# First FFN weight block of an attention and quantized-FFN kernel: four tiles converted in place and turned by transposing transfers during the last two batches

## The reference

```python
def _L0_xattn_ref(query, key):
    a = jnp.einsum('bqd,bkd->bqk', query, key)
    e = jax.nn.softmax(a, axis=-1)
    return jnp.einsum('bqk,bkd->bqd', e, key)
...
    w = _dequantize(qweight, weight_scale, weight_zero_point)   # (v - zero_point) * scale
    return jnp.einsum('bsk,nk->bsn', x, w) + bias
...
    x = x + jnp.tanh(g_xattn[0]) * _L0_xattn_ref(_layernorm(x, axis=-1), ctx_4096)
    x = x + jnp.tanh(g_ffn[0]) * _L0_ffn_ref(_layernorm(x, axis=-1), ...)
    return x
```

## Time and profile before

| | us |
|---|---|
| median of three runs | 578.82 |
| lowest, highest | 577.61, 582.05 |
| the profiled execution | 578.77 |
| its span, first to last instruction | 577.0 |
| PE busy | 565.8 (98%) |
| DVE busy | 358.7 (62%) |
| ACT busy | 287.5 (50%) |
| POOL busy | 214.7 (37%) |
| SP's queue, share of 16 DMA engines | 66.3% |

### The profile page before, as it was taken

The page is one execution under the profiler, slowest core; times in us unless marked ns, Lnnn a source line. Parts: engine busy times, 40 slices in busy tenths (PEclk is TensorE's granted clock), DMA queues, the critical chain, the costliest instruction groups (busy, mean ns, idle before and its releaser), DMA issues.

```text
span 577.0 us, 8618 instructions
## 1 busy us (share of the span) xinstructions
PE 565.8 (98%) x3390; PEld 407.1 (71%) x3390; DVE 358.7 (62%) x684; ACT 287.5 (50%) x447; POOL 214.7 (37%) x187
## 2 busy tenths in 40 slices
PE   7989999999999999999999999999999999999997
PEld 7879969968968977987986996665554444444445
DVE  5577717826836745755673782966949665655443
ACT  3667567568666676765765757545431220210000
POOL 3046178169249339429619709912000000000000
PEclk9999999999999999999999999999999999999999
DMA  7999749327828727747755675788996994962311
GB/s 237 277 321 240 215 149 305 98 81 239 255 86 274 262 84 265 257 119 220 247 173 177 246 236 229 252 304 279 243 233 208 211 260 134 196 161 71 86 55 42
DMA packets 49203, 115.79 MB, mean 201 GB/s; under 512 B 27960, under 2 KB 28216, under 8 KB 40546
## 3 DMA queue, kind: packets, MB, share of 16 engines
q1 hardware_dynamic: 49052, 114.41, 66.3%
q10 hardware_dynamic: 110, 0.82, 0.5%
HBM read 89.26 MB, written 19.66 MB: 189 GB/s over the span
## 4 chain that ended last, share of the span: by engine, by line
PE 85%; DMA 8%; DVE 5%; issue 1%; ACT 1%; SPq 0%
PE S L1161 19%; PE S L1051 13%; PE T L1005 10%; PE pv L1089 8%; PE S L1089 8%; PE S L1053 7%; PE pv L1161 7%; PE pv L1005 6%; DMA raw<-in_ctx 3%; DMA raw<-late 3%; PE pv L1102 3%; PE S L1102 3%; DVE xres L779 3%; DMA xa<-in_x 1%; DVE qT L897 1%
## 5 line engine op out<-in xcount | busy, mean ns | idle before, releaser
L505 POOL TENSOR_TENSOR vlo<-raw,vhi 128x2048 fp32r<-128x2048 f32 (+1 forms) x38 | 174.3, 4614 | 54.9 <-ACT vhi L571 54.9
L1051 PE MATMUL S<-khi,qT 128*100 128x362 f32 x512 | 141.4, 357 | 0.0
L1053 PE MATMUL S<-klo,qT 128*100 128x362 f32 x256 | 85.1, 332 | 0.3
L907 DVE TENSOR_TENSOR klo<-T,khi 128x361 fp32r<-128x361 f32 x128 | 65.9, 529 | 25.1 <-ACT khi L560 24.4
L907 DVE TENSOR_TENSOR klo<-pv,khi 128x361 fp32r<-128x361 f32 x128 | 65.2, 527 | 22.5 <-ACT khi L560 22.0
L560 ACT ACTIVATE khi<-T 128x361 fp32r<-128x361 f32 x128 | 58.6, 475 | 34.8 <-PE T L1005 34.5
L571 ACT ACTIVATE vhi<-raw 128x2048 fp32r<-128x2048 f32 (+1 forms) x38 | 71.9, 1908 | 6.9 <-PE S L1089 6.9
L560 ACT ACTIVATE khi<-pv 128x361 fp32r<-128x361 f32 x128 | 58.5, 476 | 28.3 <-PE pv L1005 28.3
L1161 PE MATMUL S<-raw 128*128 128x512 f16 x320 | 71.6, 379 | 0.0
L1005 PE MATMUL T<-ident,raw 128*128 128x128 f32 (+1 forms) x416 | 64.2, 268 | 3.8 <-DMA raw<-in_ctx 2.5
L1051 PEld LDWEIGHTS S<-khi,qT 128*100 128x100 f32 x512 | 67.7, 167 | 0.0
(11 more groups left out here) (130 smaller groups left out, 740.5 us busy)
## 6 DMA issues: line engine op xcount, KB each, us to landing
raw<-in_ctx SPq DMA_DIRECT2D x24, 1024.0 KB, 10.3
raw<-in_L_ffn_qweight SPq DMA_DIRECT2D x16, 768.0 KB, 8.2
raw<-in_ctx SPq DMA_DIRECT2D x12, 840.0 KB, 10.6
rows_scratch<-xres SPq DMA_DIRECT2D x8, 800.4 KB
xres<-in_x SPq DMA_DIRECT2D x8, 800.0 KB
x_scratch<-xres SPq DMA_DIRECT2D x8, 800.0 KB
raw<-in_ctx SPq DMA_DIRECT2D x12, 512.0 KB, 12.6
late<-x_scratch SPq DMA_DIRECT2D x24, 256.0 KB, 4.3
```

The source lines that it names most:

```text
L505: pool.tensor_tensor(vlo[0:r, k, :], raw[0:r, b % 2, t, 0:D], vhi[0:r, k, :].bitcast(F32), ALU.subtract).then_inc(s_vlo, 1)
L907: dve.tensor_tensor(klo[:, slot, 0:GW], T[k][:, 0:GW], khi[:, slot, 0:GW].bitcast(F32), ALU.subtract).then_inc(s_free[k], 1)
L1051: pe.matmul(into[0:R, g, 0:MW], qT[:, h, c, :], khi[:, slot, :], start=(c == 0 and h == 0), stop=False)
L1053: last = pe.matmul(into[0:R, g, 0:MW], qT[:, 0, c, :], klo[:, slot, :], start=False, stop=(c == CH - 1))
```

## The change

Block 0 now goes the way of the other blocks. ACT converts each of its four tiles in place, where DVE unpacked it, and SP turns it into `WT[0]` by a transposing transfer. PE's 64 transposes, their identity matrix in half precision and ACT's eight copies are gone. Tiles 2 and 3 are unpacked into the third part of `consts`, so the zero points, which belong there, are loaded only when those two tiles are turned, and DVE unpacks tile 2 ahead of the lower half of row tile 0 and tile 3 ahead of that of row tile 1. ACT converts tile 0 behind the last batch's exponentials, tile 1 behind its turned probabilities, tiles 2 and 3 on either side of the first upper half of row tile 1.

```diff
+        def unp_at(n):
+            if n in (2, 3):
+                return consts[:, 2, (n - 2) * 1024:(n - 1) * 1024].bitcast(U16).rearrange("p (j g) -> p j g", j=4)
+            return unp[n % 2]
...
         def wn_at(n):
             k = n % 2
+            if n < RT:
+                return unp_at(n).rearrange("p j g -> p (j g)").bitcast(F16)
...
+        def converted(n):
+            return n + 1
+        def turned_at(n):
+            return 16 * (n // RT + 1)
...
             def weights_turned(n):
                 nb, rt = divmod(n, RT)
-                if nb >= 2:
+                if nb == 0:
+                    used(LAST - 1, 4)
+                    used(LAST - 1, 5)
+                elif nb >= 2:
                     sp.wait_ge(s_y, (nb - 1) * MT)
-                sp.wait_ge(s_wn, n - RT + 1)
+                sp.wait_ge(s_wn, converted(n))
                 sp.dma_start_transpose(WT[nb % 2][:, :, rt * P:(rt + 1) * P], wn_at(n)).then_inc(s_wt[rt], 16)
...
-            sp.dma_start(cB, wzero.rearrange("n o -> (n o)").partition_broadcast(P)).then_inc(s_cB, 16)
             load_rows(1)
             rows_out(LAST - 2)
+            for n in range(3):
+                weights_turned(n)
             x1_out(LAST - 1)
             next_xres(LAST)
             used(LAST, 2)
             load_rows(2)
             load_w(RT)
+            weights_turned(3)
             load_rows(3)
             load_w(RT + 1)
             rows_out(LAST - 1)
+            for n in (2, 3):
+                sp.wait_ge(s_wt[n], turned_at(n))
+            sp.dma_start(cB, wzero.rearrange("n o -> (n o)").partition_broadcast(P)).then_inc(s_cB, 16)
             load_rows(4)
...
                 exps(i + 1)
+                if i + 1 == LAST:
+                    weights_exact(0)
...
                     probs(LAST)
+                    weights_exact(1)
                     ln2_norm(i - 1)
                     rows_hi(0, 1)
                 context_hi(i + 1, 1)
             context_hi(LAST, 2)
-            weights(0)
-            weights(1)
+            weights_exact(2)
             rows_hi(1, 0)
+            weights_exact(3)
             rows_hi(1, 1)
-            weights(2)
             ln2_norm(LAST - 1)
-            weights(3)
...
+                    if n in (2, 3):
+                        dve.wait_ge(s_scores, B)
+                    elif n in (RT, RT + 1):
+                        dve.wait_ge(s_wt[n - RT], turned_at(n - RT))
...
+            unpack(2)
             rows_lo(0, 0)
             probs_lo(LAST)
             rows_lo(0, 1)
             residual(LAST - 1)
             ln2_stats(LAST - 1)
-            unpack(2)
+            unpack(3)
             rows_lo(1, 0)
-            unpack(3)
             rows_lo(1, 1)
...
                 if m == 0:
-                    for f in range(2):
-                        if nb == 0:
-                            written("W", nb * RT + RT - 1, f)
-                    if nb >= 1:
-                        for k in range(RT):
-                            pe.wait_ge(s_wt[k], 16 * nb)
+                    for k in range(RT):
+                        pe.wait_ge(s_wt[k], turned_at(nb * RT + k))
...
-            attend(LAST, {0: lambda: weights(0), 1: lambda: weights(1), 2: lambda: normed(1, (0, 1)),
-                          3: lambda: normed(1, (2, 3)), 4: lambda: weights(2), 5: lambda: weights(3)})
+            attend(LAST, {2: lambda: normed(1, (0, 1)), 3: lambda: normed(1, (2, 3))})
```

More of the change, by code:

```diff
@@ L92, in flamingo_block @@
         ident = sb("ident", [P, P])
-        ident16 = sb("ident16", [P, P], F16)
         fold = sb("fold", [P, 32])
@@ L238, in flamingo_block @@
                 fill("x", 0, 2, 2)
-        for n in range(2):
-            fill("W", n, 2)
         fill("x", 1, 4)
-        for n in range(2, RT):
-            fill("W", n, 2)
         fill("x", 2, 4)
@@ L461, in _ @@
             pool.memset(ident[:, :], 0.0).then_inc(s_id0, 1)
-            pool.memset(ident16[:, :], 0.0).then_inc(s_id0, 1)
             pool.memset(half[:, :], -0.5).then_inc(s_half, 1)
[L464 to L467, removed]
+            pool.wait_ge(s_id0, 1)
+            pool.affine_select(out=ident[:, :], in_=ident[:, :], compare_op=ALU.not_equal, fill=1.0,
+                               base=0, pattern=[[-1, P]], channel_multiplier=1).then_inc(s_id, 1)
             pool.memset(fold[:, :], 0.0).then_inc(s_fold, 1)
@@ L638, in weights_exact @@
                     act.wait_ge(s_pv, B * NCH)
-                elif n not in (2 * RT, 2 * RT + 1):
-                    act.wait_ge(s_wt[(n - 2) % RT], 16 * ((n - 2) // RT))
+                elif n >= RT and n not in (2 * RT, 2 * RT + 1):
+                    act.wait_ge(s_wt[(n - 2) % RT], turned_at(n - 2))
                 act.wait_ge(s_u, n + 1)
-                act.activation(wn_at(n), unp[n % 2].rearrange("p j g -> p (j g)").bitcast(F16), ACT.Copy,
+                act.activation(wn_at(n), unp_at(n).rearrange("p j g -> p (j g)").bitcast(F16), ACT.Copy,
                                bias=-float(BIAS16)).then_inc(s_wn, 1)
@@ L826, in unpack_piece @@
                         lo_made(dve, LAST - 1, 1)
-                    if 2 <= n < RT + 2:
-                        bk, u = bank("W", n - 2, 1)
-                        dve.wait_ge(s_turned[bk], u + 1)
+                    if n in (2, 3):
+                        dve.wait_ge(s_scores, B)
+                    elif n in (RT, RT + 1):
+                        dve.wait_ge(s_wt[n - RT], turned_at(n - RT))
                     elif n >= RT + 2:
-                        dve.wait_ge(s_wn, n - 2 - RT + 1)
-                    dve.tensor_scalar(unp[n % 2][:, 1, :], p[:, :, 0, 0], 6, 63, ALU.logical_shift_right,
+                        dve.wait_ge(s_wn, converted(n - 2))
+                    dve.tensor_scalar(unp_at(n)[:, 1, :], p[:, :, 0, 0], 6, 63, ALU.logical_shift_right,
                                       ALU.bitwise_and).then_inc(s_u1, 1)
@@ L835, in unpack_piece @@
                     j, w = ((0, 0), (2, 1), (3, 2))[k - 1]
-                    dve.tensor_scalar(unp[n % 2][:, j, :], p[:, :, w, 0], 63, 0x6400, ALU.bitwise_and, ALU.bitwise_or)
+                    dve.tensor_scalar(unp_at(n)[:, j, :], p[:, :, w, 0], 63, 0x6400, ALU.bitwise_and, ALU.bitwise_or)
                 else:
                     dve.wait_ge(s_u1, n + 1)
-                    dve.tensor_scalar(unp[n % 2][:, 1, :], unp[n % 2][:, 1, :], 0x6400, None,
+                    dve.tensor_scalar(unp_at(n)[:, 1, :], unp_at(n)[:, 1, :], 0x6400, None,
                                       ALU.bitwise_or).then_inc(s_u, 1)
@@ L1117, in normed @@
                                      for j in range(n) for q, gb in [divmod(n * f + j, G4 // P)]])
-            def weights(n):
-                if n == 0:
-                    pe.wait_ge(s_id, 2)
-                pe.wait_ge(s_u, n + 1)
-                for f in range(2):
-                    k, u = bank("W", n, f)
-                    pe.wait_ge(s_free[k], u)
-                    for c in range(8 * f, 8 * f + 8):
-                        q, gb = divmod(c, G4 // P)
-                        last = pe.transpose(T[k][:, :].bitcast(F16)[:, (c % 8) * P:(c % 8 + 1) * P],
-                                            unp[n % 2][:, q, gb * P:(gb + 1) * P].bitcast(F16), ident16[:, :])
-                    last.then_inc(s_turned[k], 1)
             def multiply(nb, m, between={}):
```

4 lines of the change are left out of this document (removed).

## The result

The kernel after takes 594.32 us (median of 6 runs, 592.04 to 596.74) against 581.48 us for the kernel before beside it (577.61 to 583.13): a ratio of 1.0245, 95% interval 1.021 to 1.028, so 2.5% slower. The forecast was 592.0 us, in a range of 578 to 602: 13.3 us added to 578.8, where 12.8 were measured over 581.48. The profiled execution of after took 592.98 us with a span of 591.2.

The account below looks back on a forecast made before the run. PE and SP's DMA queue were taken as bounds. Four transfers at 3.6 us (14.4) plus 3.0 for cB less 5.1 of filled gaps gave 12.3; with 1.0 start shift, 578.8 + 13.3 = 592 us, range 578 to 602.

Parts of the forecast that it names:

- two limits: PE, busy 98% of the span, and SP's one DMA queue, side by side in the kernel before.
- Gate A: Ahead of the first FFN matmul, PE waits 7 to 11 us for all four transposing transfers of block 0.
- the walk: SP's queue followed in issue order with a price per transfer, from the load of rows 1 issued at 359.71 us.
- start shift: At the queue's start, DVE's unpacking of tile 2 and POOL's steps hold each other up: 0 to 3 us, 1.0 taken.
- Gate B: At row tile 5, ACT's conversion of tile 7 waits for its late transposing transfer; PE stands about 5 us more.
- The price of a transposing transfer: Service in SP's queue for each 512 KB transposing transfer: 3.6 us, range 2.4 to 4.0.
- cB at 3.0 us: Late 1 MB load of the zero points in SP's queue, counted as 3.0 us of added delay.
- rival 4: PE's clock falls in the new gaps, adding 2 to 5 us behind Gate B: 594 to 597 us; chance 0.13.
- The 3.5 us that PE saves: PE drops four batches of 16 transposes before the first FFN matmul, 3.5 us in all, possibly eaten by small delays.
- Hidden: SP's queue takes block 0's transfers in its free engines, so not slower: 575.3 to 574.1 us; chance 0.12.
- No dearer than plain bytes: Each transposing transfer in SP's queue costs 1.5 us, as plain bytes do: 583.7 us; chance 0.13.
- Only gate A: The queue catches up before row tile 5, so only the first FFN matmul's wait counts: 586 us; chance 0.12.

Follow-up runs that it names:

- experiment 3: Kernel after, but weight tiles 2 and 3 of block 0 turned by PE and copied by ACT again: 590.07 us, 1.0186 to before.
- experiment 8: Kernel after with the zero points loaded into 16 of 128 partitions, 128 KB instead of 1 MB: 596.69 us, 1.032 to before.
- experiment 5: Kernel after with block 0's four transposing transfers replaced by plain copies: 590.51 us with 4 KB runs, 595.15 us with 256-byte runs.
- experiments 1 and 2: Kernel after, first with ACT making row tile 5's upper halves before converting weight tile 7, 589.64 us; then with block 0's fourth transposing transfer issued earlier, 592.79 us.
- experiment 6: Kernel after with useless matmuls, 36 before block 0 and 17 at row tile 5: 595.01 us; second run, the 17 moved to where PE stands: 595.83 us.

## Why the prediction held, step by step

- **The two limits and the two gates**: right. Gate A, forecast at 7 to 11 us, is 8.45, and opens at 394.39 - 0.48 = 393.9 on before's clock, the time the walk gave for T3 (394.9 with the start shift). Gate B, forecast at some 5 us, is 4.03; T5 was to land at 434.6 + 1.0 and did at 434.8. On T5's landing and so the end the sum said 13.3; measured are 12.4 behind the mark on the landing and 1.3 for the clock.
- **The price of a transposing transfer**, 3.6 us each in a range of 2.4 to 4.0: right for the queue as a whole up to T4, but not where the walk put it. T4 lands 14.1 us later behind the mark than in before (413.17 and 427.74, less the marks), just the 13.1 of the walk and the 1.0 of the start. But T2 was issued at 371.96 and landed 4.2 us later (the shortest landing of all), so by the prices of the walk it was served until 374.3 and the queue was free of rows 1 and rows out 5 at 367.2, which leaves 7.1 us for three, 2.4 each, the lower bound. And input 7, by the same prices due at 382.4, came at 388.2, in DVE's timeline:

```profile
388.20 1.41 DVE L792 SCALAR_TENSOR_TENSOR xres<-pv,soft,xres 100x512 f32<-100x512 f32 x2 [7.13 <-DMA xres<-in_x]
```

  The delay is in the plain transfers behind. At T5 12.4 of the 14.1 us are left, 3.1 per transfer (experiment 3), where the walk kept 13.3. Why 100-row transfers behind transposing ones are slow, and why 1.7 us come back between T4 and T5, is not settled.
- **cB at 3.0 us**: wrong, it costs nothing (experiment 8). In the walk itself only 1.1 of the 3.0 were not under a wait for the store of rows 6; that wait was longer than walked, and covered all.
- **What of the sum is luck**. 14.4 + 3.0 - 5.1 came out at 12.3 with one term that is nothing; what a transfer takes and what the filled gaps give back were not measured apart, only what is left of both at T5. And the landing came 0.9 us before the sum's 13.3, while the 1.3 us of the clock, which the sum left to rival 4, were added: that the end fits to 0.4 us (13.7 against 13.3) is two errors that balance.
- **The start shift of 1.0 us**: right in size and place. The queue's store of rows 5 goes out 20.40 us behind the mark instead of 19.60, and POOL's steps of `rstd` take 0.33 to 0.40 us instead of 0.19 to 0.20 beside DVE's unpacking of tile 2, in after's timeline of POOL:

```profile
348.71 0.33 POOL L510 TENSOR_SCALAR ln<-ln 100x1 f32<-100x1 f32 x1
...
350.02 9.11 POOL L523 TENSOR_TENSOR vlo<-raw,vhi 128x2048 fp32r<-128x2048 f32 x2
```

  This low half started at 348.88 in before, so 0.66 us later behind the mark. The single step of 4.91 us in the earlier trace rows did not come here, but it came back, as 4.86 us, in the unpacking of tile 3, with row tile 1's lower half behind it, in after's timeline of DVE:

```profile
369.04 5.69 DVE L850 TENSOR_SCALAR consts<-raw 128x512 uint16<-128x512 uint16 x3
...
374.85 1.28 DVE L824 TENSOR_TENSOR raw<-T,raw 128x512 f16<-128x512 f32 x2
```

  This is the lower half for which PE waits at 375.59, as the prediction expected.
- **The 3.5 us that PE saves**: mostly gone before they could count, as the upper end of the forecast arrival (386.5) allowed. PE reaches gate A at 385.95, 1.05 us earlier behind the mark. The three waits shown above (0.29, 0.36 and 0.84 us) account for the rest: measured from the start of the row ahead of a wait to the start of the next undisturbed one, these places take 0.65, 0.52 and 1.24 us longer than in before, 2.4 in all. Under gate A none of it matters.
- **Rivals**. *Hidden* falls with the gaps; the idle third at 364 to 372 that spoke for it is a third of all 16 engines' time, so by the prediction's own 10 of 16 the other six stood nearly throughout. *No dearer than plain bytes* falls with experiment 5, where 512 KB cost 3.1 us of queue turned, 170 GB/s, and 1.75 plain. The rule of the Trainium skill behind that rival (Advanced Engine Details and Errata, X-Bar Transpose (TRN2)), transposing transfers as fast as regular ones, does not hold in this kernel's loaded queue. *Only gate A* falls with experiments 1 and 2. *The clock* came true in part: it fell in both gaps, was covered behind A, and added 1.3 us behind B, not the 2 to 5 of that rival. Around the gaps of after the granted clock was 0.76 to 0.88 of full speed over a stretch, and the second run of experiment 6, with work of no use in both gaps, shows no such slow rows behind them. The Trainium skill's page TensorE: Matmul & The Clock Gate (HAM oscillation) tells of waits for DMAs that take PE to the lower level; the trace agrees.

## What to carry to other kernels

Before taking work from a busy engine into a DMA queue, walk that queue in issue order to the first load that an engine waits for; where two limits lie within 1.2 us of each other, 3.5 us off the one are worth nothing against 12 on the other. Reordering such a queue or removing one gate can open the next one (here gate A, gate B, then weight tile 6). Compare runs from a mark behind the part that varies, and check a sum's terms one by one, since two wrong ones can balance.

## What was not expected of the hardware

- SP was held long by a transposing transfer behind a loaded queue: 2.29 us for T2 and 12.76 for T3 in after, and 8.09 us for two plain copies in runs of 256 bytes, against 1.43 for two in runs of 4 KB.
- At gate B the ten matmuls took 3.06 us behind a gap of 4.03 (after), 4.01 behind 4.04 (short runs), 4.40 behind 4.21 (two turned) and 2.32 behind 1.52 (plain copies): gaps of nearly the same length gave slow stretches of different length. Behind the 3.05 us of gate A with T3 earlier they took 2.32.
- A copy handed over in 0.47 us landed some 13 us later (experiment 5): how long SP was held did not tell when it would land.
